# State of linear attention in four diagonal 32x32 blocks on column tiles, with one column of ones for the key sums

## The reference, cut to what matters

```python
qkv = jnp.einsum('btc,ec->bte', x, Wqkv).reshape(b, t, 3, H, D)     # H = 16 heads, D = 8
q, k, v = qkv[:, :, 0], qkv[:, :, 1], qkv[:, :, 2]
q = elu(q) + 1.0
k = elu(k) + 1.0
kv    = jnp.einsum('bnhd,bnhm->bhdm', k, v)          # the state: one 8x8 matrix per head and sequence
k_sum = k.sum(axis=1)
out   = jnp.einsum('bnhd,bhdm->bnhm', q, kv)
out   = out / (jnp.einsum('bnhd,bhd->bnh', q, k_sum) + EPS)[..., None]
out   = out @ Wproj.T + bproj
```

## Time and profile before

| | |
|---|---|
| median of 3 runs | 678.49 us |
| the profiled execution, its own time | 678.38 us |
| its span, first to last instruction | 676.6 us |
| mean granted TensorE clock | 0.985 |
| PE busy with matmuls / with weight loads | 623.5 us (92%) / 409.5 us (61%) |
| DVE, ACT, POOL busy | 419.6 us, 427.1 us, 308.8 us |
| chain that ended last: PE, DVE, ACT | 88%, 5%, 3% |

### The profile page before, as it was taken

The page is one execution under the profiler, slowest core; times in us unless marked ns, Lnnn a source line. Parts: engine busy times, 40 slices in busy tenths (PEclk is TensorE's granted clock), DMA queues, the critical chain, the costliest instruction groups (busy, mean ns, idle before and its releaser), DMA issues.

```text
span 676.6 us, 14602 instructions
## 1 busy us (share of the span) xinstructions
PE 623.5 (92%) x5140; PEld 409.5 (61%) x5140; DVE 419.6 (62%) x1114; ACT 427.1 (63%) x585; POOL 308.8 (46%) x585
## 2 busy tenths in 40 slices
PE   0847698999999999999999999999999999999986
PEld 0633354656575766757585757667575857575855
DVE  2356556677767666676667676666766676674340
ACT  0302275666868768685868687686858686868341
POOL 6002408164645354654546453546545464446332
PEclk9977899999999999999999999999999999999999
DMA  5500101101011110101111111101001111000001
GB/s 164 190 16 9 33 13 29 21 20 22 21 21 36 18 39 12 42 8 19 33 21 37 21 36 19 39 13 42 9 19 32 22 36 34 8 1 16 16 17 31
DMA packets 31671, 20.96 MB, mean 31 GB/s; under 512 B 9328, under 2 KB 27504, under 8 KB 31600
## 3 DMA queue, kind: packets, MB, share of 16 engines
q1 hardware_dynamic: 31600, 20.03, 12.1%
HBM read 9.53 MB, written 4.19 MB: 20 GB/s over the span
## 4 chain that ended last, share of the span: by engine, by line
PE 88%; DVE 5%; ACT 3%; issue 2%; SPq 1%; DMA 1%; POOL 0%; DVEq 0%; ACTq 0%
PE ring L475 18%; PE ring L465 17%; PE ps_t L443 8%; PE ring L403 8%; PE ps_s L427 8%; PE ring L452 5%; PE ring L484 4%; PE ring L500 4%; PE ps_s L422 3%; PE ring L508 2%; PE ring L535 2%; PE ring L524 2%; PE ring L514 2%; PE ring L491 2%; PE ps_t L562 1%
## 5 line engine op out<-in xcount | busy, mean ns | idle before, releaser
L814 DVE TENSOR_REDUCE rowmax<-ps_s 128x16 f32<-128x1024 f32 x64 | 78.0, 1219 | 39.6 <-PE ps_s L427 39.5
L679 ACT ACTIVATE probs_t<-ps_t 128x1024 f32<-128x1024 f32 x64 | 65.5, 1023 | 29.5 <-PE ps_t L443 29.0
L819 DVE TENSOR_TENSOR shifted<-ps_s,rowmax 128x1024 f32<-128x1024 f32 x64 | 78.4, 1225 | 7.0 <-PE ps_t L443 0.5
L671 ACT ACT_TABLE_LOAD x57 | 73.1, 1283 | 8.7 <-PE ring L465 7.9
L443 PE MATMUL ps_t<-ident,shifted 128*128 128x128 f32 x512 | 68.7, 278 | 3.3 <-DVE shifted L819 3.3
L679 ACT ACT_TABLE_LOAD x42 | 53.9, 1283 | 26.2 <-PE ps_t L443 26.2
L427 PE MATMUL ps_s<-kx,q_t 64*32 64x512 f32 x1024 | 70.2, 618 | 0.0
L465 PE MATMUL ring<-xT_G,w1b 128*128 128x512 f32 x128 | 67.4, 613 | 2.3 <-ACT xT_G L663 1.0
L443 PEld LDWEIGHTS ps_t<-ident,shifted 128*128 128x128 f32 x512 | 58.5, 143 | 12.6 <-issue 9.1
L475 PEld LDWEIGHTS ring<-w,hid_G 128*128 128x128 f32 x512 | 58.4, 192 | 9.5 <-issue 4.9
L475 PE MATMUL ring<-w,hid_G 128*128 128x128 f32 x512 | 61.2, 278 | 2.8 <-ACT hid_G L671 2.8
(11 more groups left out here) (120 smaller groups left out, 1205.6 us busy)
## 6 DMA issues: line engine op xcount, KB each, us to landing
kx<-kv_t SPq DMA_DIRECT2D x256, 20.0 KB
x_P<-in_x SPq DMA_DIRECT2D x16, 256.0 KB, 2.9
out_x<-x_G SPq DMA_DIRECT2D x16, 256.0 KB, 3.2
vx_t<-kv_t SPq DMA_DIRECT2D x128, 8.0 KB
up_s<-in_up_m SPq DMA_DIRECT2D x7, 256.0 KB, 5.6
down_s<-in_down_m SPq DMA_DIRECT2D x7, 256.0 KB, 5.6
u_t<-in_w_exp_t SPq DMA_DIRECT2D x1, 258.0 KB, 3.7
vx_t<-in_vones_c SPq DMA_DIRECT2D x1, 256.0 KB, 2.9
```

Source lines behind the costliest of these rows:

```text
L671: nc.scalar.activation(hid[s][:, c], bank(name)[:], ACT.Gelu, bias=b1[:, c:c + 1]).then_inc(drained[BANK[name]].sem, 1)
L679: nc.scalar.activation(probs_t[:, j % 2], ps_t[:], ACT.Exp).then_inc(drained["T"].sem, 1)
L814: nc.vector.tensor_reduce(rowmax[:, j], s, AX_X, ALU.max).then_inc(vec.sem, 1)
L819: nc.vector.tensor_tensor(shifted[:, j % 2].rearrange("p h k u -> p k h u"), ps_s[:].rearrange("p k (h u) -> p k h u", u=SPAN), m, ALU.sub ...
```

## The change

`v_ext` holds each tile of values in four quarters of 32 columns, each with one column of ones behind it (33 columns). `linear_state` makes, for each tile of rows, four matmuls of 32 key features by 33 columns in place of one of 128 by 144; the output of quarter c goes to partitions 32c to 32c+31, so it lies on column tile c of the array. What is outside the diagonal 32x32 blocks isn't computed. The 33 columns of a sequence hold, in every partition, the quarter that belongs to this partition, and the key sum. `linear_state_out` spreads this back to 128 and 16 columns: one DVE operation reads the 32 columns four times over and multiplies by the mask, a second one reads the key sum 16 times over and multiplies by the mask's last 16 columns. ACT writes v into the new layout.

```diff
+QUARTERS = 4
+QW = DIM // QUARTERS
+VW = QW + 1
-        v_ext = sb("v_ext", [P, TILES, KVW])
+        v_ext = sb("v_ext", [P, TILES, QUARTERS, VW])
...
                         j = TPB * b + i
-                        last = nc.tensor.matmul(bank("L.kv")[:, KVW * b:KVW * (b + 1)], phi_k[:, j], v_ext[:, j],
-                                                start=(i == 0), stop=(i == TPB - 1))
+                        for c in range(QUARTERS):
+                            rows = slice(QW * c, QW * (c + 1))
+                            last = nc.tensor.matmul(bank("L.kv")[rows, VW * b:VW * (b + 1)], phi_k[:, j, rows],
+                                                    v_ext[:, j, c], start=(i == 0), stop=(i == TPB - 1))
                 last.then_inc(product.sem, 1)
...
-                nc.scalar.activation(v_ext[:, 2 * m:2 * m + 2, 0:DIM], kv[:, :, P:2 * P], ACT.Copy)
+                nc.scalar.activation(v_ext[:, 2 * m:2 * m + 2, :, 0:QW],
+                                     kv[:, :, P:2 * P].rearrange("p j (c n) -> p j c n", c=QUARTERS), ACT.Copy)
...
+                made = bank("L.kv")[:, 0:GB * VW].rearrange("p (b a n) -> p b a n", b=GB, a=1)
+                same = kvmask[:, 0:DIM].rearrange("p (a c n) -> p a c n", a=1, c=QUARTERS)
                 nc.vector.tensor_tensor(
-                    kvs[:], bank("L.kv")[:, 0:GB * KVW].rearrange("p (b n) -> p b n", b=GB),
-                    kvmask[:].rearrange("p (a n) -> p a n", a=1).to_broadcast([P, GB, KVW]), ALU.mult
+                    kvs[:, :, 0:DIM].rearrange("p b (c n) -> p b c n", c=QUARTERS),
+                    made[:, :, :, 0:QW].to_broadcast([P, GB, QUARTERS, QW]),
+                    same.to_broadcast([P, GB, QUARTERS, QW]), ALU.mult)
+                nc.vector.tensor_tensor(
+                    kvs[:, :, DIM:KVW], made[:, :, 0, QW:VW].to_broadcast([P, GB, HEADS]),
+                    kvmask[:, DIM:KVW].rearrange("p (a n) -> p a n", a=1).to_broadcast([P, GB, HEADS]), ALU.mult
                 ).then_inc(drained[BANK["L.kv"]].sem, 1)
```

## The result

The changed kernel takes 672.16 us (median of 4 runs, 671.87 to 673.26) where the kernel before takes 679.16 us (median of 4, 678.38 to 680.63). The ratio is 0.9897, 95% interval 0.9875 to 0.992, that is 1.0% faster, 7.0 us. Forecast were 671.7 us and a gain of 6.7 us.

The account below looks back on a forecast made before the run. PE's instructions were taken to bound the full turn. Gains of 14 x 0.452 + 0.402 = 6.7 us from the profiled 678.4 us gave 671.7 us; eight-in-ten range 670.4 to 675.4 us.

Parts of the forecast that it names:

- PE bounds the turn, and only it: Full turn of 37.12 us: PE busy for 37.09 us, so any shorter PE instruction shortens the turn.
- Four tiles side by side, weights loaded behind: State matmuls: 8 rounds of four column tiles, loads hidden; piece 0.378 us instead of 0.98 us; full overlap given 62%.
- Rival 1: State matmuls: weight load and stream in series, 0.054 us a round; gain 3.9 us, 674.5 us; chance 17%.
- rival 2: State matmuls: a tile's two records stay together, 16 steps of 0.030 us; 675.2 us; 11% together with half a gain.
- the estimate of 0.05 us a round: State matmuls: about 60 cycles minimum for each of two passes per float32 record would make a round 0.05 us.
- A round is 0.030 us, by the stream of 33 columns: State matmuls: 0.0021 us fixed plus 33 columns at 0.00084 us each; 8 rounds take 0.24 us.
- Way in and out, 0.29 us a visit: Around the state: changing to column tiles costs 0.138 us, changing back into the transposes 0.15 us.
- Net 0.452 us a turn: State and transposes behind: 0.602 us gained, 0.15 us lost on the way out, in each of 14 turns.
- DVE costs nothing: State read-out on DVE: two operations, 0.61 us instead of 0.46, the extra 0.15 us covered by its wait.
- ACT writes v in quarters: Writing v_ext: as many values as before, a gap every 32, readers 20 us away.
- The slower rival, supply of instructions: State matmuls: PE's instruction stream limits 32 pairs at 0.055 us each; 16 us slower, 694 us; chance 7%.
- the eight pairs of L422: Argument on instruction supply: in the densest stretch these pairs ran in 0.22 us, so at least 24 instructions were ready.

Follow-up runs that it names:

- e6: Changed kernel with 9 columns streamed in place of 33 in each state matmul, same weights; one run, 672.8 us, against the changed kernel's 672.16 us.
- e4: Changed kernel with the state made in two visits, the second amid the eight transposes of the last probabilities; 0.9969 of the time before the change.
- e9: e7 with POOL's bias addition of stage L moved behind that of stage P; 0.9939 of the time before the change, full turn 36.69 us.
- e7: Changed kernel with DVE's masked spread made three times, 0.85 us more DVE work a turn; 0.997 of the time before the change.
- e5: Changed kernel with the state's matmuls made four times over in one visit, 128 pairs; one run, 690.2 us, against the changed kernel's 672.2 us.
- e8: Changed kernel with the state moved between the third scores and weighted values, beside other column tiles, and read out earlier; 666.94 us, 0.9827 of before.

## Why the prediction was right

- *PE bounds the turn, and only it.* Held: a full turn got shorter by 0.43 to 0.44 us, and the pieces of L529 and L446 account for it.
- *Four tiles side by side, weights loaded behind.* Held. Piece 0.39 us for 0.378 forecast. Rival 1 (0.57 us by its rounds of 0.054) and rival 2 (0.62 us) fall by the piece, and so does the estimate of 0.05 us a round that stood beside rival 1's bound.
- *A round is 0.030 us, by the stream of 33 columns.* The size was right (0.032 us), the reason was not: e6 streams 9 columns and its rounds are 0.032 us as well. The forecast chose L475 as its row because load and stream are equally long in both, and that choice would cover a pace set by the load. It doesn't cover the issue of four pairs; if that sets the pace, the size was luck.
- *Way in and out, 0.29 us a visit.* Held, read from another line (L452) and shown by e4.
- *Net 0.452 us a turn.* 0.44 us measured; the missing 0.01 us lies in the rounds, which take about 0.0015 us each more than forecast.
- *DVE costs nothing.* True for full turns of the changed kernel, but in the first turn with a state the chain runs through both of its operations (0.42 and 0.10 us), and e9 shows that in the turns with stages missing longer work there isn't covered. The reason given was incomplete, too. I looked at what waits for DVE, and at POOL's queue only for being late; e7 and e9 show that what a POOL operation collides with when it is late counts too. The change used DVE's cover to within 0.15 us of that collision.
- *ACT writes v in quarters.* No ACT piece that writes v entered the chain in a full turn. The one ACT piece there, `xT_G` in a single turn, stands in the chain before as well.
- *The slower rival, supply of instructions.* Not met at 32 or 64 pairs; unevenness begins behind some 75 pairs (e5). Its cause stays open. One argument against it doesn't come out: the eight pairs of L422 that ran through in 0.22 us show 16 instructions ready, not the 24 that it names.

## What to carry to other kernels

When one engine's pieces fill the turn without a gap, a change on it can be priced from pieces of the same kind in the same trace, the neighbours' included, here to 0.01 us a turn: two fifths of what the change should have saved (0.74 us by columns, 0.44 us net) went into changing the array's tiling and back. So put small tiled matmuls next to others with the same tiling, and into a wait that exists anyway; in e8 that was worth 0.51 us in most turns, 0.24 us by the neighbours and 0.27 us by the wait, more than the 0.35 us of the four tiles where they stood first. The bank it needed for this cost a wait in one turn. A price from the full turn doesn't hold for the first and last turns, where another engine can be the one behind which PE waits. And when work on DVE grows, check which POOL operations it pushes, and which two-input DVE operations these would meet.

## What was not expected of the hardware

- Matmuls on column tiles with 9 and with 33 columns cost nearly the same, 0.37 and 0.39 us for 8 rounds of four with the way in, and their rounds are 0.032 us apart in both; the stream isn't what limits them.
- Most visits of 128 small pairs have gaps of 0.1 to 0.2 us near their 78th and their 122nd matmul, two of the 16 have none, and visits of 32 and 64 pairs have practically none.
- A DVE multiplication with both inputs in SBUF took 0.59 us in place of 0.29 while a POOL addition with both inputs in SBUF was running, and 0.29 us again in every full turn once that addition had been moved (e9).
